# Block 2's neighbour sum over 64 units, block 3's attention terms from Ws times a, and the back's layer normalisations in pairs of tiles

## The reference

```
# block 2
h = relu(x @ W1 + b1) @ W2 + b2            # W1 512x64, W2 64x512
agg = segment_sum(h[dst], src)             # the sum over a node's neighbours
x = layernorm(x + h + agg)
# block 3, for each of 8 heads
Wx = x @ Ws[h] + Wb[h]                     # Ws[h] 512x64
s = Wx[dst] @ a_w[h, :64] + Wx[src] @ a_w[h, 64:] + a_b[h]
alpha = softmax over the edges of one dst of leaky_relu(s)
out[dst] = sum of alpha * Wx[src]
x = layernorm(x + out)
```

## Time and profile before

| | us |
|---|---|
| median of three runs | 1427.46 |
| lowest, highest | 1423.25, 1427.70 |
| the profiled execution | 1433.77 |
| its span | 1432.0 |

### The profile page before, as it was taken

The page is one execution under the profiler, slowest core; times in us unless marked ns, Lnnn a source line. Parts: engine busy times, 40 slices in busy tenths (PEclk is TensorE's granted clock), DMA queues, the critical chain, the costliest instruction groups (busy, mean ns, idle before and its releaser), DMA issues.

```text
span 1432.0 us, 15034 instructions
## 1 busy us (share of the span) xinstructions
PE 1184.3 (83%) x5694; PEld 893.7 (62%) x5694; DVE 868.3 (61%) x1523; ACT 455.3 (32%) x670; POOL 282.7 (20%) x325
## 2 busy tenths in 40 slices
PE   5977935557978998899889998899889999784883
PEld 2644612224547986797669877798679867344552
DVE  6686834334647255667656656667666644667885
ACT  1112810000004452346234343236234422203881
POOL 1155048888801001100110000000110000112001
PEclk9998966677989999799999999999999999796997
DMA  5234745432012231221110201121010313000001
GB/s 171 65 100 134 241 139 127 107 76 53 5 67 97 82 95 56 76 86 34 30 59 1 96 24 59 30 78 42 30 59 1 102 39 87 0 0 0 1 1 36
DMA packets 47735, 92.58 MB, mean 65 GB/s; under 512 B 17167, under 2 KB 17567, under 8 KB 46375
## 3 DMA queue, kind: packets, MB, share of 16 engines
q1 hardware_dynamic: 27170, 70.40, 15.3%
q0 software_dynamic: 20480, 20.99, 6.2%
HBM read 73.29 MB, written 17.91 MB: 64 GB/s over the span
## 4 chain that ended last, share of the span: by engine, by line
PE 59%; DVE 18%; POOL 8%; issue 6%; ACT 5%; DMA 3%; SPq 0%; DVEq 0%; POOLq 0%; ACTq 0%
PE ps L1503 13%; PE ps L1450 12%; PE ps L1478 9%; PE ps L1483 5%; POOL arena L563 4%; POOL logit_ring L569 4%; PE ps L1635 4%; PE ps L1466 3%; PE ps L1607 3%; PE ps L1537 3%; DMA logits_scratch<-arena 2%; PE ps L1583 2%; DVE arena L1405 2%; DVE arena L1404 2%; DVE arena L1170 1%
## 5 line engine op out<-in xcount | busy, mean ns | idle before, releaser
L1450 PE MATMUL ps<-arena 125*128 125x314 f32 (+3 forms) x768 | 211.3, 432 | 3.6 <-ACT arena L658 3.4
L1607 PE MATMUL ps<-arena 125*125 125x512 f32 x192 | 136.8, 808 | 91.2 <-DVE arena L1038 74.1
L545 POOL TENSOR_TENSOR var_eps<-mean_var,ln_consts 125x1 f32<-125x1 f32 x70 | 17.4, 248 | 881.5 <-DVE mean_var L1156 582.6
L1450 PEld LDWEIGHTS ps<-arena 125*128 125x128 f32 (+3 forms) x768 | 135.8, 180 | 69.5 <-ACT arena L658 3.6
L569 POOL DMA_INDIRECT logit_ring<-logits_scratch,pair_idx x80 | 103.1, 1288 | 88.0 <-DMA logits_scratch<-arena 64.0
L563 POOL DMA_INDIRECT arena<-value_scratch,src_idx x80 | 104.8, 1310 | 41.1 <-issue 23.7
L1537 PE MATMUL ps<-ident,arena 125*125 125x125 f32 x625 | 80.9, 283 | 27.0 <-ACT arena L846 15.2
L1537 PEld LDWEIGHTS ps<-ident,arena 125*125 125x125 f32 x625 | 75.7, 194 | 34.9 <-ACT arena L846 17.2
L1607 PEld LDWEIGHTS ps<-arena 125*125 125x125 f32 x192 | 37.1, 241 | 93.7 <-issue 93.5
L1608 PEld LDWEIGHTS ps<-arena 125*125 125x125 f32 x192 | 45.2, 235 | 64.7 <-issue 64.7
L1478 PE MATMUL ps<-input_high,weight_high 128*128 128x314 f32 x320 | 73.0, 309 | 2.3 <-DVE weight_low L1140 2.3
(11 more groups left out here) (246 smaller groups left out, 2703.7 us busy)
## 6 DMA issues: line engine op xcount, KB each, us to landing
logits_scratch<-arena SPq DMA_DIRECT2D x5, 2187.5 KB
arena<-in_m_w SPq DMA_DIRECT2D x8, 1024.0 KB, 6.5
arena<-in_w_up SPq DMA_DIRECT2D x4, 1024.0 KB, 5.2
arena<-in_w_down SPq DMA_DIRECT2D x4, 1024.0 KB, 7.5
arena<-in_wq SPq DMA_DIRECT2D x4, 1024.0 KB, 5.2
arena<-in_wk SPq DMA_DIRECT2D x4, 1024.0 KB, 5.2
arena<-in_wv SPq DMA_DIRECT2D x4, 1024.0 KB, 5.2
arena<-in_wo SPq DMA_DIRECT2D x4, 1024.0 KB, 5.4
```

The costliest lines, as they stand in the source:

```text
L1450: last = mm(out_view[:, place:place + HALF_W], w, r[:, lo:lo + HALF_W], start=n == 0, stop=n == len(pairs) - 1)
L1607: mm(ps[0:TILE, 512 * j:512 * j + 512], onehot, VG[slot][:, u, :], start=False, stop=True, skip_group_check=True)
```

## The change

- Block 2: the hidden units are made as rows, 125 nodes by 64 units, tile by tile; the bias comes in by a matmul. A 65th column of ones is added (`HIDR`). The neighbour sum is taken over these 65 columns, and an identity adds each node's own row, so that one product with `W2`, under which `b2` stands as a 65th row, gives h + agg. DVE adds it to `X`.
- Block 3's attention terms: `Ws` times `a_w`, summed over a head's 64 columns, gives 16 columns (`WA`), made on DVE after each hidden tile of the last layer (`head_weights`). PE multiplies the turned tiles by them (`fg`, high and low parts) with a constant row from `Wb`, `a_w` and `a_b`. The first terms are turned into columns (`fcol`), the second are spread by a pick matrix (`PICKG`), one product for each head. `wx` comes after the first two heads' rows.
- `norm` in front of blocks 2 and 3 becomes `back_norm`: a pair of tiles (two, two, one) is added and normalised before the next pair is added. PE turns each tile when it is ready.
- All banks of the back are in the plan `B`. `Ws` is loaded into the third weight buffer when `o` is done, `a_w` when the last attended head is done.

```diff
@@ sync @@
+                if i == LAYERS - 1:
+                    B.wait_filled(sp, ("av", i, H1 - 1))
+                    load(AW, aw3.partition_broadcast(128), "aw")
                 B.wait_filled(sp, ("o", i, 2))
...
-                    load(AW, rows3.partition_broadcast(TILE), "aw")
+                    load(WS3, feat_view(ws3), "ws3")
                 B.wait_filled(sp, ("m1", i, FT - 1))
...
-                    load(WS3, feat_view(ws3), "ws3")
                     sp.wait_ge(sig("x1_stored"), 32)
                     node_transfer(XIN, rows_view(x1_d), "ld_x1")
@@ gpsimd @@
+            B.wait_filled(pool, ("m1", LAYERS - 1, FT - 1))
+            g.tensor_copy(PICKG, ident[0:2 * H3, H3:2 * H3].unsqueeze(2).to_broadcast([2 * H3, H3, TILE])).then_inc(sig("pick_ready"), 1)
...
-                    g.tensor_tensor(PRODG[:, t, :], V[:, t, :], AW[:, 1, :], ALU.mult).then_inc(sig("g_products"), 1)
...
-                g.tensor_copy(g_bc[:, :, :], gcol[:, :, h:h + 1].to_broadcast([TILE, NT, TILE])).then_inc(sig("g_spread"), 1)
@@ scalar @@
+                if i == LAYERS - 1:
+                    act.wait_ge(sig("wa_ready"), 1)
+                    a.activation(WAH[:, :, :], WA.rearrange("p k s h -> p k (s h)"), ACT.Copy).then_inc(sig("wa_high"), 1)
+                    one_weight_high("ws3", WS3, WS3_SLOT)
...
+            for t in range(NT):
+                B.wait_filled(act, ("t", 2, t))
+                B.release(("t", 2, t), a.activation(YT[:, :, TILE * t:TILE * (t + 1)], B.blocks(("t", 2, t), FT, 128), ACT.Copy))
+            B.wait_filled(act, ("hid",))
+            act.wait_ge(sig("ones_ready"), 1)
+            B.release(("hid",), a.activation(HIDR[:, :, 0:HID2], B.view(("hid",))[:, 0:NT * HID2].rearrange("p (t c) -> p t c", t=NT), ACT.Relu))
+            B.wait_filled(act, ("agg",))
+            B.release(("agg",), a.activation(halves(AGT), B.halves(("agg",), HID2 + 1), ACT.Copy))
             act.wait_ge(sig("lc2_half"), 1)
             a.activation(LC, LC, ACT.Ln).then_inc(sig("ln_done"), 1)
...
+            B.wait_filled(act, ("fg",))
+            B.release(("fg",), a.activation(halves(FG), B.halves(("fg",), 2 * H3), ACT.Copy))
+            B.wait_evacuated(act, ("fcol",))
@@ vector @@
+            def head_weights(k):
...
+                for side in range(2):
+                    dve_chain(dve, v.tensor_tensor(WA_PROD, WS3[:, k, :], AW[:, side, :], ALU.mult))
+                    last = v.tensor_reduce(WA[:, k, side, :], WA_PROD.rearrange("p (h d) -> p h d", h=H3), AX.X, ALU.add)
+                    dve_chain(dve, last)
...
+                    if i == LAYERS - 1:
+                        head_weights(f)
...
+            v.tensor_tensor(WAL[:, :, :], WA.rearrange("p k s h -> p k (s h)"), WAH[:, :, :].bitcast(f32), ALU.subtract).then_inc(sig("wa_low"), 1)
+            one_weight_low(2, WS3, WS3_SLOT)
+            dve.wait_ge(sig("ld_x1"), 32)
+            def back_norm(base, pair, done):
+                for t in pair:
+                    dve_chain(dve, v.bn_stats(stats[:, t, :], X[:, t, :]))
+                    v.bn_aggr(mv[:, t, :], stats[:, t, :]).then_inc(sig("var_ready3"), 1)
+                for t in pair:
+                    dve.wait_ge(sig("rstd_ready3"), base + t + 1)
+                    v.tensor_scalar(X[:, t, :], X[:, t, :], mv[:, t, 0:1], rstd[:, t:t + 1],
+                                    ALU.subtract, ALU.mult).then_inc(sig(done), 1)
             for n, pair in enumerate(PAIRS):
+                tiles = slice(pair[0], pair[-1] + 1)
                 mid_add(("m2", LAYERS - 1, n), pair)
+                dve_chain(dve, v.tensor_tensor(X[:, tiles, :], X[:, tiles, :], XIN[:, tiles, :], ALU.add))
...
+                back_norm(0, pair, "xn_ready3")
             dve.wait_ge(sig("ld_c2"), 32)
             make_log_counts(C2, "lc2_half")
             dve.wait_ge(sig("ln_done"), 2)
             dve_chain(dve, v.tensor_tensor(LC, LC, LTMP["lc2_half"], ALU.add))
+            for n, pair in enumerate(PAIRS):
+                tiles = slice(pair[0], pair[-1] + 1)
+                B.wait_filled(dve, ("h", n))
+                B.release(("h", n), v.tensor_tensor(X[:, tiles, :], X[:, tiles, :], B.view(("h", n)).rearrange("p (b c) -> p b c", c=D),
+                                                    ALU.add))
...
+                back_norm(NT, pair, "xn_ready3")
...
             masked3(0)
+            for n, pair in enumerate(PAIRS):
+                row_bias(B, ("wx", n), pair, V, ROWS[:, 0:1, :])
@@ tensor @@
+            turn_node(("t", 2, 0), 0, 1)
+            for t in range(1, NT):
+                turn_node(("t", 2, t), t, t + 1)
+                hidden_rows(t - 1)
+            B.fill(hidden_rows(NT - 1))
...
+            wide(B.view(("agg",), HID2 + 1), [(HIDR[:, k, :], C2[:, k, :]) for k in range(NT)], open_end=True)
...
+                        last = mm(B.view(("agg",), HID2 + 1)[:, place + first:place + last_], HIDR[:, t, :],
+                                  ident[0:TILE, first - TILE * t:last_ - TILE * t], start=False,
+                                  stop=last_ == min(hi, NODES))
...
+            all_rows(B, "h", AGT.unsqueeze(1), cw2[:, :].unsqueeze(1), 1)
+            for t in range(NT):
+                turn_node(("t", 3, t), t, NT + t + 1)
...
+            for c in range(FT):
+                for w in (WAH, WAL):
+                    for place, lo in ((0, 0), (512, HALF_W)):
+                        mm(view[:, place:place + HALF_W], w[:, c, :], YH[:, c, lo:lo + HALF_W], start=False, stop=False)
+            B.wait_evacuated(pe, ("t", 3, NT - 1))
...
             def g_rows(h):
+                B.claim(pe, ("g", h))
+                B.fill(wide(B.view(("g", h)), [(PICKG[:, h, :], FG)]))
             g_rows(0)
             g_rows(1)
+            pe.wait_ge(sig("lone_weight_low"), 2)
+            split_rows(B, ("wx",), YH, YL, WHIGH[WS3_SLOT], WLOW[WS3_SLOT])
```

More of the change, by code:

```diff
@@ L815, in _ @@
                     input_high(i + 1, 1)
-            for k in range(0, FT, 2):
-                C.wait_filled(act, ("t", 2, k))
-                C.release(("t", 2, k), a.activation(tiled(YT[:, k, :]), C.blocks(("t", 2, k), NT, 128), ACT.Copy))
-            C.wait_filled(act, ("hid",))
-            C.release(("hid",), a.activation(halves(HID2T), C.halves(("hid",), HID2), ACT.Relu, bias=col("c_b1", 0, HID2)))
+            for t in range(NT):
+                B.wait_filled(act, ("t", 2, t))
+                B.release(("t", 2, t), a.activation(YT[:, :, TILE * t:TILE * (t + 1)], B.blocks(("t", 2, t), FT, 128), ACT.Copy))
@@ L1328, in _ @@
                         weight_low("wq", i + 1)
+                    if i == LAYERS - 1:
+                        head_weights(f)
                 if i < LAYERS - 1:
                     mid_norm(i + 1, 1, "m2", i)
+            back = (sig("var_ready3"), sig("rstd_ready3"), sig("xn_ready3"))
+            dve.wait_ge(sig("ld_rows3"), 16)
+            dve.wait_ge(sig("ld_c"), 64)
+            for side in range(2):
+                dve_chain(dve, v.tensor_tensor(WA_PROD[0:1, :], ROWS[0:1, 0, :], AW[0:1, side, :], ALU.mult))
+                dve_chain(dve, v.tensor_reduce(CONST_FG[:, H3 * side:H3 * (side + 1)], WA_PROD[0:1, :].rearrange("p (h d) -> p h d", h=H3),
+                                               AX.X, ALU.add))
@@ L1450, in wide @@
                         last = mm(out_view[:, place:place + HALF_W], w, r[:, lo:lo + HALF_W],
-                                  start=n == 0, stop=n == len(pairs) - 1)
+                                  start=n == 0, stop=n == len(pairs) - 1 and not open_end)
                 return last
@@ new lines, in _ @@
+            B.fill(last)
+            B.wait_evacuated(pe, ("agg",))
+            all_rows(B, "h", AGT.unsqueeze(1), cw2[:, :].unsqueeze(1), 1)
+            for t in range(NT):
+                turn_node(("t", 3, t), t, NT + t + 1)
+            B.claim(pe, ("fg",))
+            pe.wait_ge(sig("const_ready"), 1)
+            pe.wait_ge(sig("wa_low"), 1)
+            view = B.view(("fg",), 2 * H3)
+            for place, lo in ((0, 0), (512, HALF_W)):
+                mm(view[:, place:place + HALF_W], CONST_FG, ONES[:, lo:lo + HALF_W], start=True, stop=False)
@@ new lines, in _ @@
+            pe.wait_ge(sig("back_high"), NT)
+            for c in range(FT):
+                for w in (WAH, WAL):
+                    for place, lo in ((0, 0), (512, HALF_W)):
+                        mm(view[:, place:place + HALF_W], w[:, c, :], YH[:, c, lo:lo + HALF_W], start=False, stop=False)
+            B.wait_evacuated(pe, ("t", 3, NT - 1))
+            for c in range(FT):
+                for place, lo in ((0, 0), (512, HALF_W)):
+                    last = mm(view[:, place:place + HALF_W], WAH[:, c, :], YL[:, c, lo:lo + HALF_W], start=False, stop=c == FT - 1)
@@ new lines, in _ @@
+            B.fill(last)
+            B.claim(pe, ("fcol",))
+            B.wait_evacuated(pe, ("fg",))
+            for t in range(NT):
```

(7 more changed lines are left out.)

234 lines of the change are left out of this document (105 added, 129 removed).

## The result

The changed kernel took 1415.14 us (median of 6 runs, 1408.21 to 1417.28) against 1427.06 us of the old one (6 runs, 1423.25 to 1429.92): a ratio of 0.9913, interval 0.9894 to 0.9932, 11.9 us faster, which is clear of no difference but less than 2%. Forecast were 1406 us and a gain of 21.7. The profiled execution took 1414.86 us (span 1413.0), 18.9 less than the old profiled one. So there are two misses: 3 us inside the changed stretch, and the step from a profiled execution to the medians.

A forecast was written before the change was run, and what follows sets the result against it. Bound, from 1223 us on, by one chain of waits through PE, DVE, ACT and POOL. Heads start 20.9 us earlier and the loop saves 0.8: 21.7 off the 1427.46 median, forecast 1406 us, range 1396 to 1418.

The forecast's parts named there:

- step 2: First back normalisation by pairs: ends at 1235.3 against 1235.45, no gain, 2 us either side.
- Step 3: Block 2's hidden layer by rows: 2.8 us after the last tile's transposes, relu 0.5, ending at 1239.8.
- Step 4: Neighbour sum over 64 units: 8.5 us (7.2 to 13.1) with identity pieces, ending at 1248.3.
- 5 logarithm, `LC`: Before block 2's output addition: DVE newly waits for ACT's logarithm, then adds to `LC`, until 1256.8; gives back 5 us.
- 6 second norm: Second back normalisation, by pairs: 13.3 us, ending at 1270.1 (old: 1278.76).
- Step 7: Block 3's attention terms: 10.7 us, so edge sums begin at 1280.8, 25.7 us earlier.
- 8 `wx`, heads: Start of the head loop: set by `wx`, not the exponentials, at 1297.9, 20.9 us earlier.
- Step 9: Head loop: first transposes faster with PE hot from `wx`, -0.8 us (0 to -1.3); longer head rows absorbed by idle time.
- rival A: PE stays at its lower clock through the back stages: some +7 us, 1413; chance 0.15.
- Step 1: Head weights and constants on DVE: hidden under m2's matmuls at no cost, DVE free at 1218.8.
- Rival C: DVE's block of head weights and constants outlasts its cover, by slower products or late `WS3`: +4 us, 1410; chance 0.07.
- D: Head loop becomes bound by PE as its clock falls; slower than before, up to +64 us, 1470; chance 0.03.

The follow-up runs named there:

- e_best3: e_best with 36 small added matmuls, results unread, keeping PE busy in gaps of the back stages; 1400.25 us, ratio 0.9804 to the old kernel.
- e_block: Changed kernel with DVE's head constants and low head weights moved behind the log-count scalings; 1409.51 us, ratio 0.9872 to the old kernel.
- After: First profile of the changed kernel, unaltered; 1414.86 us, span 1413.0.
- a_again: Changed kernel, unaltered, profiled again; 1414.92 us.
- a_last: Changed kernel, unaltered, measured and profiled once more beside the old kernel; 1413.55 us, ratio 0.9895.
- b_again2: Old kernel, unaltered, in its third profile; 1426.09 us.
- first profile of before: Old kernel, unaltered, the profile on which the forecast rests; 1433.77 us, span 1432.0.
- b_again: Old kernel, unaltered, profiled a second time; 1430.76 us.
- e_wxshort: Changed kernel with two of the three products of block 3's `wx` left out, 20 of 60 matmuls staying; 1411.05 us.
- e_ln: Changed kernel with DVE's wait for block 2's logarithm and the addition to `LC` moved behind the second norm; 1410.8 us, ratio 0.9886 to the old kernel.
- e_best: Changed kernel with the moves of e_ln and e_block, plus the attention terms' constant row ahead of the last turn; 1399.29 us, ratio 0.980 to the old kernel.

## Why the prediction was right and wrong

The median lies between the 1396 and 1418 forecast, 9 us above the 1406, and the order of events was right: which wait ends last at each step, `wx` under the edge sums, DVE waiting for the logarithm. By its own steps, the new trace on the old axis (0.43 us added, so that the marks stand together; 1.25 would make PE's ends of m2 meet, and then step 2 is 0.8 slower than shown and the loss 3.9):

| step | predicted end | measured end | the step itself |
|---|---|---|---|
| 2 first norm | 1235.3 | 1233.6 | -1.7 |
| 3 hidden rows, relu | 1239.8 | 1240.8 | +2.7 |
| 4 neighbour sum | 1248.3 | 1250.3 | +1.0 |
| 5 logarithm, `LC` | 1256.8 | 1258.6 | -0.2 |
| 6 second norm | 1270.1 | 1271.0 | -1.0 |
| 7 attention terms | 1280.8 | 1282.1 | +0.4 |
| 8 `wx`, heads | 1297.9 | 1299.7 | +0.5 |
| 9 loop | -0.8 | +0.5 | +1.3 |

Unrounded, the column sums to 3.1: the gain behind the layers is 18.6 us, not 21.7.

- Step 3 failed in its price and its model. Two tiles were counted behind the last turn at 0.3 a matmul. A tile's four take 1.94 at the lower clock, recorded as 8, so 0.48 each, above the upper bound of 0.42; and with 2.95 us a tile PE's queue, not the norm, became the bound, so the 1.7 us that step 2 won are lost here. The row:

```profile
1237.83 1.94 PE L1830 MATMUL ps<-c_w,arena 128*125 128x64 f32 x8
```

- Step 4 was mis-sized by 1.0: its ten matmuls took 8.35 us where 6.7 was taken, by the old hidden layer's 0.67 each, and the identity pieces 1.10 for 1.8. The granted clock was 0.69. It is rival A in one place. At the full clock (e_best3) it would have been 1.9 below the forecast.
- Step 7 missed the constant row, 2.2 us on the chain behind the last turn (L1861), because ACT's copy was thought to set the start; the matmuls behind it were cheaper than assumed.
- Step 1 failed in its cover. What it calls costing nothing, the slip of the hidden tiles, cost PE nothing (25.06 against 25.02 us, above). But the cover was judged by m2's last addition, at 1223.04, while the new order begins the norm with the first, and DVE could make that one long before, in the old trace already:

```profile
1213.26 1.22 DVE L1182 TENSOR_TENSOR arena<-arena,ps 125x1024 f32<-125x1024 f32 x1 [4.04 <-PE ps L1503]
```

In the new trace PE has m2's first pair done at 1211.98 and the block holds its addition until 1217.75; without the block the heads begin 3.0 us earlier (e_block). The sum was not hurt, since step 2 starts from the block's end at 1218.8 (1218.2 on that axis).
- Step 9 came out at +0.5, +0.5 and -0.8 in the three profiles of the changed kernel. Its size is within what the loop does by itself: 112.3 to 115.0 over the ten profiles that share it. After and a_again have a granted clock of 0.83 from 60 to 70 us into it, a_last 1.00.

The larger miss is the last line, the step from the profiled execution to the median: 1427.46 - 21.7. That takes the median execution's back to be that of the profiled one and its excess of 6.31 us to be met again, or not, alike in both kernels. Laid against each other, b_again2 (1426.09 us, near the old median) and a_again (1414.92, near the new) are 11.2 apart: 18.7 behind the layers (222.8 by the first profile of before, 204.1), less 2.6 because b_again2's sum had the full clock, less 4.9 because its layers ended at 1204.09 and not at 1209.03. Of the 4.9, 0.8 is the moved mark, with which the 18.7 is as much too large; 3.4 stands at the first `o` product (426.17 and 429.60), and the rest in between. So the forecast took from the median a saving that was measured against a slow sum, and gave the changed kernel the median execution's block 0, where its own three profiles had a later one. This is one pair of profiles, chosen by their times; another, b_again and a_last, is 15.0 apart in span. What makes block 0 late in one execution and not in the next was not isolated, nor whether the changed program's is later for a reason, nor what calls the clock's dips.

Rival A's 1413 lies nearer to the median than the forecast, but not for its reasons: of its 7 us step 4 brought 1.0 and step 7, priced at 1.3, 0.4. Rival C came in one instruction: a head-weight product took 1.19 us where its like take 0.69, while POOL's pick copy ran (1205.67 to 1206.68); DVE was free at 1217.75 all the same. D did not come: the loop's clock stayed at 0.96.

## What to carry to other kernels

When work is cut out of a chain, ask of each instruction put into an engine's queue what is ready behind it: one moved wait, one moved block and one moved row were worth about as much again as the change itself kept (26.9 us in all, against 11.9 and 14.3). And price a step with the clock that PE may have after the cut: here the sum's matmuls, 32 records in place of 50, ran at 0.69, and the old ones at 0.89 or 1.00. Subtract a predicted gain from a median only after seeing, in a second profile, how the stretches ahead of the change and in it vary, and count from a mark that the change itself doesn't move.

## What the runs showed of the hardware that was not expected

- Four f32 matmuls of 64 columns took 1.08 to 1.09 us at the full clock and 1.94 at the lower, recorded as 8: 0.27 and 0.48 each, where 64/314 of the 0.67 of the earlier trace rows is 0.14.
- A one-partition f32 matmul of 314 columns, two of them in four records, took 2.27 us at the lower clock and 1.23 at the full one (e_best3): 0.61 each there, where the sum's ten over 125 partitions took 5.51, or 0.55 each.
- The head loop took 114.6 to 115.0 us in e_wxshort, e_ln and e_best3, where time won ahead of it came back only in part, and in each the granted clock dipped early: 0.76 in its first 20 us in e_wxshort (0.91 in a_again), 0.83 from 20 to 40 us in e_ln and e_best3 (1.00 in e_best). In e_block, which began it 3.0 us earlier too, it took 112.54. So an earlier start does not by itself lengthen the loop; what calls the dips is open.
